# Router logits by groups of 32 tokens turned by VectorE, and the routing's transpose at the front of the block

## What is computed

```python
out = jnp.einsum('boi,bih->boh', agg_w, x) + agg_b[:, :, None]     # y: the batch's 64x64 mixing
router_logits = xf @ gate_w.T                                      # xf = y; 8 experts
routing = softmax(router_logits, axis=1)
in_scale = routing @ in_channel_scale
out_scale = routing @ out_channel_scale
out = xf * in_scale @ sign(weight).T * out_scale + bias
x = x + out
```

## Time and profile before

| | |
|---|---|
| median of 3 runs | 541.09 us (540.41 to 542.42) |
| the profiled execution | 541.51 us |
| its span, first to last instruction | 539.7 us |
| granted TensorE clock, mean | 0.999 of full |
| layer 0's large matmuls, from the first to the last | 20.4 to 190.4 us |

### The profile page before, as it was taken

How to read it: one execution, slowest core, us unless ns; L and a number is a source line. 1 busy time by engine, 2 the same in 40 slices (tenths; PEclk the granted TensorE clock), 3 DMA queues, 4 the chain that set the end, 5 groups by cost and what they waited for, 6 DMA issues and landing times.

```text
span 539.7 us, 14212 instructions
## 1 busy us (share of the span) xinstructions
PE 523.5 (97%) x5717; PEld 446.1 (83%) x5717; DVE 301.5 (56%) x482; ACT 121.6 (23%) x291; POOL 253.3 (47%) x121
## 2 busy tenths in 40 slices
PE   5897999999999999999999999999999999999997
PEld 4675778788787898898988988989889889898895
DVE  4579998797775654447446354364453634734411
ACT  5733334444434330101101011010010110101100
POOL 0028766766767398154263360651623616426100
PEclk9999999999999999999999999999999999999999
DMA  8696455554667362532413414224143162251111
GB/s 304 230 403 226 164 194 175 204 204 167 194 221 231 110 211 84 123 108 56 147 66 110 128 47 145 98 63 149 52 120 118 42 159 85 76 145 55 40 40 39
DMA packets 55049, 74.68 MB, mean 138 GB/s; under 512 B 6192, under 2 KB 41200, under 8 KB 55024
## 3 DMA queue, kind: packets, MB, share of 16 engines
q1 hardware_dynamic: 54800, 73.96, 42.4%
q10 hardware_dynamic: 224, 0.36, 0.3%
HBM read 57.50 MB, written 16.79 MB: 138 GB/s over the span
## 4 chain that ended last, share of the span: by engine, by line
PE 92%; DVE 4%; ACT 2%; issue 1%; DMA 1%; SPq 0%; DVEq 0%; ACTq 0%
PE bank L639 54%; PE bank L525 19%; PE bank L620 5%; PE bank L682 4%; PE bank L451 3%; PE bank L464 2%; PE bank L498 2%; DVE parts L978 1%; PE bank L601 1%; DVE y_t L949 1%; DMA cst<-in_consts 1%; ACT late L754 1%; PE bank L474 0%; PE bank L481 0%; DVE y_t L971 0%
## 5 line engine op out<-in xcount | busy, mean ns | idle before, releaser
L639 PE MATMUL bank<-early,parts 128*128 128x320 f32 (+1 forms) x1152 | 206.7, 337 | 0.0
L639 PEld LDWEIGHTS bank<-early,parts 128*128 128x128 f32 x1152 | 184.6, 188 | 16.6
L525 PE MATMUL bank<-late,parts 128*128 128x512 f32 x512 | 129.5, 403 | 2.1 <-DVE work L986 2.1
L525 PEld LDWEIGHTS bank<-late,parts 128*128 128x128 f32 x512 | 93.3, 190 | 23.0 <-DVE work L986 2.9
L1222 POOL TENSOR_TENSOR xs<-raw 128x1024 f32<-128x1024 f32 x14 | 26.5, 1894 | 157.1 <-DMA raw_turned<-x_scratch 157.1
L978 DVE TENSOR_TENSOR parts<-y_t,parts 128x512 fp32r<-128x512 f32 x64 | 95.0, 1503 | 2.5 <-ACT parts L785 1.0
L639 PE MATMUL bank<-late,parts 128*128 128x512 f32 x384 | 94.1, 394 | 0.0
L639 PEld LDWEIGHTS bank<-late,parts 128*128 128x128 f32 x384 | 70.9, 188 | 15.9
L1170 POOL TENSOR_TENSOR work<-work 128x512 f32<-128x512 f32 x32 | 46.3, 1448 | 47.3 <-DVE work L986 46.1
L1114 DVE TENSOR_TENSOR qk<-bank,qk 128x256 f32<-128x256 f32 x16 | 6.8, 424 | 102.1 <-ACT qk L874 102.1
L785 ACT ACTIVATE parts<-y_t 128x512 fp32r<-128x512 f32 x62 | 38.5, 631 | 88.3 <-DVE y_t L1093 46.1
(11 more groups left out here) (111 smaller groups left out, 484.7 us busy)
## 6 DMA issues: line engine op xcount, KB each, us to landing
xs<-in_x SPq DMA_DIRECT2D x16, 512.0 KB, 3.3
work<-in_x SPq DMA_DIRECT2D x16, 512.0 KB, 3.3
x_scratch<-work SPq DMA_DIRECT2D x16, 512.0 KB, 3.0
raw<-x_scratch SPq DMA_DIRECT2D x128, 64.0 KB, 2.9
work<-x_scratch SPq DMA_DIRECT2D x16, 512.0 KB, 3.6
out_tokens<-work SPq DMA_DIRECT2D x15, 512.0 KB, 2.7
raw_turned<-x_scratch SPq DMA_DIRECT2D x112, 64.0 KB, 2.5
stage<-in_wearly SPq DMA_DIRECT2D x8, 576.0 KB, 4.0
```

Of the source, the lines that this page charges most:

```text
L525: last = mm(bank[4 + h][:, :], parts[:, p, a, c, :], signs[:, c, h * HALF:(h + 1) * HALF], start=(k % 16 == 0), stop=(k % 16 == 15))
L639: return mm(dst, parts[:, p, a, c, :], w(b, c), start=(k == 0), stop=(close and k == 23))
```

## The change

`product_logits` gets one matmul for each chunk and each group of 32 tokens: 32 stationary columns as before, 32 tokens moving, written to partitions 32t onward for token group t, and all eight chunks are added up in place. `sum_logits` and `copy_logits` go, and so does the selector. VectorE turns the four 32x32 blocks of bank 2 with one transpose into the new tile `logits` in SBUF (`turn_logits`), from which `route_max` and `gate_exps` read. In `period0` the turning of the routing moves from k = 7 to the front of the block before k = 18. VectorE now has `mix_kernels` ahead of `split_routing`, and `turn_logits` behind that; ScalarE has `copy_out_scale(i, p, 1)` ahead of `round_routing`. The order in the prologue is adapted. The selector's eight columns leave the constants.

```diff
 def product_logits(i, p, first_tile=False):
     pe.wait_ge(y_biased, 4 * i + 2 * p + 2)
     if not first_tile:
-        pe.wait_ge(gate_exp, 2 * i + p)
+        pe.wait_ge(u_ready, 4 * i + 2 * p - 3)
     for c in range(L8):
-        at = slice(EP * (c % 4), EP * (c % 4) + EP)
-        made = mm(bank[2][at, 0:P], cst[:, C_GATE + c * EP:C_GATE + (c + 1) * EP], y_t[:, p, c, :],
-                  start=(c < 4), stop=(c >= 4))
+        for t in range(P // EP):
+            tokens = slice(EP * t, EP * t + EP)
+            made = mm(bank[2][tokens, 0:EP], cst[:, C_GATE + c * EP:C_GATE + (c + 1) * EP], y_t[:, p, c, tokens],
+                      start=(c == 0), stop=(c == L8 - 1))
     made.then_inc(logits_made, 1)
-def sum_logits(i, p, first_tile=False):
-    pe.wait_ge(logits_copied, 2 * i + p + 1)
-    if not first_tile:
-        pe.wait_ge(u_ready, 4 * i + 2 * p - 1)
-    mm(bank[2][:, 0:E], logits_t[:, :], cst[:, C_SEL:C_SEL + E], start=True, stop=True).then_inc(logits_done, 1)
...
-def product_scales(i, p, first_tile=False, copied=1):
+def product_scales(i, p, first_tile=False, turned=1):
     pe.wait_ge(routing_split, 2 * i + p + 1)
-    pe.wait_ge(logits_copied, 2 * i + p + copied)
+    pe.wait_ge(logits_turned, 2 * i + p + turned)
...
 def period0(i, p, one, two=None, three=None):       # TensorE
     for k in range(32):
-        if k == TURN_AT:
-            turn_routing(*one)
         if k == BLOCK_AT:
             if three:
                 inputs_of_y(*three)
+            turn_routing(*one)
             if two:
                 product_logits(*two)
             if three:
                 product_y(*three)
-            product_scales(*one, copied=2 if two else 1)
-        if k == SUM_AT and two:
-            sum_logits(*two)
+            product_scales(*one, turned=2 if two else 1)
         ffn0_step(i, p, k)
...
 for k in range(32):                                  # TensorE, tile 0
     if k == 6:
         pe.wait_ge(u_ready, 1)
-        product_logits(0, 1)
+        product_logits(0, 1, True)
     if k == 10:
         inputs_of_y(1, 0)
-        sum_logits(0, 1)
         product_y(1, 0)
...
-        product_scales(0, 1, copied=2)
-    if k == 28:
-        sum_logits(1, 0)
+        product_scales(0, 1, turned=2)
     ffn0_step(0, 0, k, True)
...
-def copy_logits(i, p):                               # ScalarE
-    act.wait_ge(logits_made, 2 * i + p + 1)
-    do(logits_t[:, :], bank[2][:, 0:P], ACT.Copy).then_inc(logits_copied, 1)
...
 def period0(i, p, one, two=None, chunk=None):        # ScalarE
+    copy_out_scale(i, p, 1)
     if one:
         round_routing(*one)
-    copy_out_scale(i, p, 1)
     if chunk is not None:
         round_stage(0, NW, (chunk + 1) * 16, early[:, 0, bass.ds(chunk, 1), :].rearrange("p a n -> p (a n)"))
-    if two:
-        copy_logits(*two)
...
+def turn_logits(i, p, first_tile=False):             # VectorE
+    dve.wait_ge(logits_made, 2 * i + p + 1)
+    if not first_tile:
+        dve.wait_ge(gate_exp, 2 * i + p)
+    v.transpose(logits[:, :], bank[2][:, 0:EP]).then_inc(logits_turned, 1)
...
 def period0(i, p, before, one, two=None, three=None, four=None):   # VectorE
     scale_out(*before, 1)
-    split_routing(*one)
     if four:
         mix_kernels(*four)
+    split_routing(*one)
+    if two:
+        turn_logits(*two)
     scale_out(i, p, 0)
```

More of the change, by code:

```diff
@@ L52 @@
 C_W1, C_W2, C_CW = 162, 290, 298
-C_GATE, C_ID, C_SEL = 362, 618, 746
-C_RLO, C_SLO, C_SSG = 754, 755, 756
-C_END = 757
+C_GATE, C_ID = 362, 618
+C_RLO, C_SLO, C_SSG = 746, 747, 748
+C_END = 749
 PRODUCTS = ((0, 0), (0, 1), (1, 0))
-TURN_AT, BLOCK_AT, SUM_AT, CONV0_AT = 7, 18, 26, 4
+BLOCK_AT, CONV0_AT = 18, 4
 LORA_AT = 11
@@ L105, in adaln_ffn_kernel @@
         gate = sb("gate", [P, 64])
-        logits_t = sb("logits_t", [P, P])
+        logits = sb("logits", [P, EP])
         qk = sb("qk", [P, 2, NQK // 2])
@@ L173, in adaln_ffn_kernel @@
         logits_made = sem("logits_made")
-        logits_copied = sem("logits_copied")
-        logits_done = sem("logits_done")
+        logits_turned = sem("logits_turned")
         gate_max = sem("gate_max")
@@ L534, in _ @@
             product_logits(0, 0, True)
-            sum_logits(0, 0, True)
             inputs_of_y(0, 1)
@@ L761, in _ @@
             take_signs(2)
-            def copy_logits(i, p):
-                act.wait_ge(logits_made, 2 * i + p + 1)
-                do(logits_t[:, :], bank[2][:, 0:P], ACT.Copy).then_inc(logits_copied, 1)
             def gate_exps(i, p):
                 act.wait_ge(gate_max, 2 * i + p + 1)
-                do(gate[:, 8:16], bank[2][:, 0:E], ACT.Exp, bias=gate[:, 0:1], accum_out=gate[:, 1:2]).then_inc(gate_exp, 1)
+                do(gate[:, 8:16], logits[:, 0:E], ACT.Exp, bias=gate[:, 0:1], accum_out=gate[:, 1:2]).then_inc(gate_exp, 1)
             def spread_routing(i, p):
@@ L805, in round_u @@
                 round_parts(i, p, y_t[:, p], u_ready, u_hi, by_block)
-            copy_logits(0, 0)
             gate_exps(0, 0)
@@ L822, in _ @@
             copy_out_scale(0, 0, 1, False)
-            copy_logits(0, 1)
             gate_exps(0, 1)
@@ L827, in _ @@
             round_routing(0, 1)
-            copy_logits(1, 0)
             round_u(0, 1, True)
@@ L950, in add_mix_bias @@
                                     row_bc[:, p:p + 1, tokens].broadcast_to([P, L8, S]), ALU.add).then_inc(y_biased, 1)
+            def turn_logits(i, p, first_tile=False):
[3 more added lines that the diff above has]
+                v.transpose(logits[:, :], bank[2][:, 0:EP]).then_inc(logits_turned, 1)
             def route_max(i, p):
-                dve.wait_ge(logits_done, 2 * i + p + 1)
-                v.tensor_reduce(gate[:, 0:1], bank[2][:, 0:E], AX.X, ALU.max, negate=True).then_inc(gate_max, 1)
+                dve.wait_ge(logits_turned, 2 * i + p + 1)
+                v.tensor_reduce(gate[:, 0:1], logits[:, 0:E], AX.X, ALU.max, negate=True).then_inc(gate_max, 1)
             def route_sum(i, p):
@@ L997, in _ @@
                                    ALU.mult, ALU.add).then_inc(scale_ready, 1)
+            turn_logits(0, 0, True)
             route_max(0, 0)
@@ L1010, in _ @@
             mix_kernels(1, 0)
+            turn_logits(0, 1)
             route_max(0, 1)
@@ L1015, in _ @@
             split_routing(0, 1)
+            turn_logits(1, 0)
             scale_out(0, 0, 0)
@@ L1262, in lay_out @@
     consts[:, C_GATE:C_ID].reshape(P, L8, EP)[:, :, 0:E] = turned(f["L0_ffn_gate_w"])
-    consts[:, C_SEL:C_SEL + E] = np.arange(P)[:, None] % EP == np.arange(E)[None]
     consts[:, C_ID:C_ID + P] = np.eye(P, dtype=np.float32)
```

## The result

The changed kernel takes 548.28 us in the median of 4 runs (547.11 to 548.4), the kernel before 541.75 us beside it (540.41 to 542.79): the ratio is 1.0118, 95% interval 1.0096 to 1.0141. It is slower by about 6.5 us, where 541.1 was forecast, with a range from 537.6 to 546.0. The profiled execution took 548.29 us, 546.5 of them span, 6.8 more than before.

What follows compares the result with a forecast made beforehand. TensorE, busy 97% of the span, was taken as the bound; -1.4 - 0.2 - 0.44 + 0.6 + 0.6 + 0.9 = 0.06, that is nothing, gave a 541.1 us median (541.5 profiled), range 537.6 to 546.

Steps and rivals of the forecast that it cites:

- The front gives nothing: Before 30 us: some 0.7 us and more won for tile 0 is lost waiting for tile 3's x, landing at 30.0.
- two signs of being wrong: Steady state: a period over 10.3 would refute the logits' price, waits before the scales (line 498) the order's.
- Small sum and logits: Each steady period on TensorE: dropping the sum saves 0.22 us, the 32-column logits cost 0.10 more, taking 0.67.
- Rival 1: Logits in the twelve periods: 32-column fours take 0.058 like 64-column ones, 0.42 a period more, about +4, 545.1; chance 0.2.
- rival 2: Logits: narrow matmuls start one by one instead of sharing the array, 1.25 a period more, some +14, 555; chance 0.05.
- The turn: Routing's turn on TensorE, moved to the block's front: costs 0.11 us there as at k = 7, nothing gained.
- rival 3: VectorE and ScalarE order becomes the bound: split and transpose late every other period, 0.4 in six, +2.4 and up; chance 0.1.
- The -0.2 at 43.61: TensorE's wait for the logits copy at 43.61 us becomes one for split and transpose, ending at 43.4.
- the waits at 56 and 77 (+0.6 each): In two blocks VectorE's split and transpose end after TensorE arrives, at 56.3 and 77.0 us: 0.6 more each.
- The wait at 72.59 (-0.44): The turn's wait for the routing at 72.59 us goes, as the routing is long there at k = 18: 0.44 saved.
- the -0.12 of every period: Net saving in a period where TensorE never waits, over twelve blocks -1.4 us.
- The last block (+0.9): Layer 0's last block: nothing stands between turn and scales, so TensorE stands still 0.9 us longer.

Runs made afterwards that it cites:

- experiment 3: Changed kernel with the routing's turn and the VectorE and ScalarE orders put back as before, only the new logits kept: 546.12 us, ratio 1.0083.
- experiment 5: Changed kernel with 92 more small matmuls, results unused, at its start (5.4 us): 547.57 us, ratio 1.0111.
- experiment 9: Kernel before with 92 more small matmuls, results unused, at 23.8 us behind tile 1's logits: 546.14 us, ratio 1.0076.
- experiment 4: Kernel before with only the routing's turn and the new VectorE and ScalarE orders, old logits kept: 543.67 us, ratio 1.0035.
- experiment 7: Changed kernel with VectorE's making of the filter taps moved behind layer 0's loop: 547.13 us, ratio 1.0091.
- experiment 10: Changed kernel with old turn and orders, 16-matmul logits for tiles 0 to 2, and taps made behind layer 0: 544.30 us, ratio 1.0050.
- experiment 6: Changed kernel with logits of tiles 0 to 2 made by 16 matmuls each instead of 64, y stationary: 545.77 us, ratio 1.0104.
- experiment 11: Same as experiment 10, with tile 3's logits also made by 16 matmuls: 542.83 us, ratio 1.0009.
- experiment 8: Kernel before with VectorE's making of the filter taps moved behind layer 0's loop: 538.93 us, ratio 0.9960.
- experiment 12: Kernel before with taps made behind layer 0's loop and 92 more small matmuls at 5.4 us: 538.06 us, ratio 0.9942.

## Why the prediction was wrong, step by step

**The step that failed is "The front gives nothing".** It took the front as bound by the load of x of tile 3 and concluded that TensorE's work before 30 us could change freely. It had no term for what 48 more matmuls and 48 more weight loads a tile ask of TensorE's instruction supply. In the changed kernel that load lands at 30.47 and the block begins at 34.88, so it no longer bounds anything. The front didn't give nothing, it took 7.0 us by 84 us: three stops of 3.53, 1.48 and 0.93, 1.50 for the lower clock behind the first, 0.76 for that behind the wait at 58.85 (2.54 - 1.78), and 1.08 more in this wait. That is 9.3; off it go 0.4 for the gap that the kernel before has as well, 0.4 for the earlier beginning at 25.42, and 1.3 and 0.6 won back at 48.37 and 84.05, so 6.6 of the 7.0 are named. Experiments 3, 5 and 9 show the stops to come from instruction counts and where they fall in time, not from order; experiment 9 loses 5.0 us by them, with about one microsecond of the padding's own work in it. No run takes the stops away and keeps the rest, so the sum above rests on the rows of one execution. The kernel before showed the thing in small: its 0.37 gap inside a mixing, with "issue" as its releaser, lay between two of the rows that I used, and I read over it. Neither of the two signs of being wrong that the prediction names (a period over 10.3, waits before the scales in the steady periods) came; both look at the steady state alone.

**Small sum and logits: right.** 0.69 against 0.67, or (0.69 - 0.16) / 16 = 0.033 for a four of 32 columns. Experiment 3 has -0.12 a period, the forecast's own figure; that the logits hit so closely is partly luck, since 0.030 a four was simply taken between 0.026 and 0.035. Rival 1 (0.058 a four) and rival 2 (one by one, 1.82) are refuted by that row. By it the Trainium skill's "TensorEngine Tiling (Array Packing)", Instruction Overhead, which lets a matmul of 32 free columns cost as much as one of 60, is contradicted here where four strips share the array.

**The turn: right.** Experiment 4's periods stay at 10.12 to 10.17.

**The order on VectorE and ScalarE (rival 3): a small part came.** In three of the eight periods the scales start 0.16 late. The rival had 0.4 in every other one. This is part of why the eight periods gain 0.72 together and not the 0.96 that eight times 0.12 make.

**The -0.2 at 43.61 and the waits at 56 and 77 (+0.6 each): not seen as such.** The first block's lateness was overrun by the stops, so the sum there says nothing about them. At 84.05, the block that answers to 77.03, TensorE didn't wait at all. In experiment 7, where the other wait is gone, there is 1.09 for the transpose at 59.58. The mechanism is real; its size in the changed kernel can't be read off.

**The wait at 72.59 (-0.44): right.** The period that answers is 9.95 instead of 10.58, -0.63; with the -0.12 of every period, -0.56 was priced.

**The last block (+0.9): right.** It is 1.02 from turn to scales. Timeline of TensorE after, answering to the earlier trace rows:

```profile
173.63 0.33 PE L490 MATMUL bank<-routing_t,scale_w 32*128 32x128 f32 x2 [0.36 <-DVE routing_t L946]
...
181.62 0.27 PE L473 MATMUL bank<-cst,routing 128*128 128x128 f32 x1
182.64 0.33 PE L490 MATMUL bank<-routing_t,scale_w 32*128 32x128 f32 x2 [0.75 <-DVE routing_t L946]
```

The block before has the wait of about 0.4 (0.36). Layer 1 moved as a whole: 6.61 later at its start, the span 6.8 longer.

**The range.** From 84.05 to layer 1's start the changed kernel takes 112.82 us, where the kernel before takes 113.23 from 77.03: 0.41 less. The terms priced for that stretch, nine periods of -0.12 and the +0.9, give some -0.2. So what was priced there came out within 0.3 us, and the whole miss lies ahead of it. The range ended at 546.0 because every rival was an event of the steady state or of an engine's list. None of them was a cost of the front.

## What to carry to other kernels

Where an edit multiplies the instructions of an engine, count them against time in the stretch where the DMA engines are full, not only in the steady loop. Look for gaps in the middle of a group, with "issue" as releaser and no semaphore wait in the program, and for the instruction queue's packets beside them. A short gap of this kind before the change is a warning: it can grow when instructions are added ahead of it (0.37 to 2.58 in experiment 9) or when the transfer comes later (1.50 in experiment 4), and taking away a wait elsewhere can bring the next one out (experiments 7 and 10). Its length differs a lot between executions, so compare medians of many runs and more than one trace before a part of it is put down to an edit.

## What the runs showed of the hardware

- TensorE's stops lie at records 449, 705, 961, 1217, 1729 and 1985, or one behind, in ten kernels (the two and eight of the experiments), always 256 or a multiple apart, whatever instruction stands there (mixing, logits or scales). They end 1.2 to 1.6 us after an instruction transfer of 16 KB ends, which itself takes 0.9 to 1.6 us. The steady loop, which comes back over the same instructions, shows no such stop in any of these kernels, and no transfer of that queue lies between 75.6 and 164.9 us in the changed one; the 64-matmul logits are cheap there (0.69) and dear in front.
- With the same program on every engine up to that place, the first stop is 3.53, 1.20 and 4.38 us long (the changed kernel, experiments 3 and 7); its transfer ends at 28.36, 26.30 and 28.76.
- When a block is asked for isn't shown. From TensorE's record 449, the entry into the block before, to the end of the transfer for record 705 are 4.4 us in the kernel before (25.99 to 30.39), 3.9 in experiment 9 (24.03 to 27.98) and 8.6 in the changed kernel (19.75 to 28.36), so the entry alone doesn't time it. No run measured the request by itself.
- The granted clock fell to 0.50 after some stops and waits: 3.53 and 2.76 in the changed kernel, 3.28 in experiment 3, 1.50 in experiment 4, 2.58 in experiment 9. It stayed full after others: 1.48 in the changed kernel, a wait of 2.83 in experiment 6. Behind the 3.53, twelve large matmuls cost 4.61 instead of 3.11; in experiment 3 the lower level lasts 6.8 us, and seventeen large matmuls take 5.87 (37.85 to 43.72) where experiment 11 has 4.01 (39.01 to 43.02). So a stop can cost 1.5 us and more on top of its length.
- The runs of experiments 7 and 9 spread by 4.2 and 6.3 us, and the 31 runs of the kernel before beside experiments 9 to 12 by 4.8 (539.83 to 544.61). The mean granted clock goes with it: the four of the 31 with 0.994 take 543.4 to 544.6 us, the 22 with 0.999 or more 539.8 to 542.3. Experiments 8 and 12, without the wait of 1.68 at 54 us, have no run below 0.999 and spread by 1.1 and 2.2. How much of the rest is the stops' varying length isn't shown.
- Left open: why the half pace of the start lasts to 33.2 us in experiment 11, and what times the instruction transfers.
